# Second-order attention: decayed states read as 32x32 tiles by TensorE instead of as spread 128x128 matrices

## The reference, cut to what matters

```python
def step(carry, qkv):
    S_K, C_QV, G = carry
    C_prev = GAMMA * C_QV
    k_C = jnp.einsum('bhk,bhkv->bhv', k_t, C_prev)
    G = GAMMA * G + k_t[..., :, None] * k_C[..., None, :]
    S_K = GAMMA * S_K + k_t[..., :, None] * k_t[..., None, :]
    C_QV = C_prev + q_t[..., :, None] * v_t[..., None, :]
    S_C = jnp.einsum('bhij,bhjv->bhiv', S_K, C_QV)
    o_t = jnp.einsum('bhk,bhkv->bhv', q_t, S_C - G)
```

## Time and profile before

| | |
|---|---|
| time, median of 3 runs | 3729.63 us |
| span of the profiled execution | 3729.0 us |
| the stage's steady part (1527 to 2762 us) | 1235 us |
| TensorE busy in it | 1226.45 us |
| VectorE, ScalarE, GpSimd busy in it | 599.01, 576.27, 566.54 us |
| TensorE busy over the whole span | 3451.4 us (93%) |

### The profile page before, as it was taken

One profiled execution on the slowest core, in us unless ns is written; L12 is line 12 of the kernel. 1 busy time (PEld: TensorE's weight loads), 2 busy tenths in 40 slices (PEclk: granted clock), 3 DMA queues, 4 the chain that ended last, 5 costly groups with the idle time before them and its releaser, 6 DMA issues. The chain is left out here.

```text
span 3729.0 us, 116380 instructions
## 1 busy us (share of the span) xinstructions
PE 3451.4 (93%) x44854; PEld 3093.9 (83%) x44854; DVE 2374.2 (64%) x6504; ACT 2169.2 (58%) x6623; POOL 1557.1 (42%) x2326
## 2 busy tenths in 40 slices
PE   8939999799839999899999999999988999999998
PEld 8929999677639999798999999999976777777777
DVE  6565555788765554555444444444446899999997
ACT  5546555455346555444444444444444888888896
POOL 5745555200035655344444444444445222222215
PEclk9969999999869999999999999999998999999999
DMA  4153343411153434200000000000000000000002
GB/s 124 47 173 84 86 94 81 121 47 58 52 195 88 94 84 91 77 3 3 3 3 3 3 3 3 3 3 3 3 6 16 2 2 2 2 2 2 2 2 96
DMA packets 137880, 164.78 MB, mean 44 GB/s; under 512 B 11376, under 2 KB 127232, under 8 KB 137344
## 3 DMA queue, kind: packets, MB, share of 16 engines
q1 hardware_dynamic: 112768, 123.79, 10.3%
q0 software_dynamic: 24576, 33.57, 5.3%
HBM read 97.16 MB, written 60.16 MB: 42 GB/s over the span
## 5 line engine op out<-in xcount | busy, mean ns | idle before, releaser
L2374 ACT ACTIVATE wa_S<-wa_S,wa_top 128x256 f32<-128x256 f32 x1024 | 512.2, 507 | 105.9 <-DVE wa_top L2442 104.9
L1956 DVE TENSOR_TENSOR so_raw<-so_rows,so_masks 128x1024 f32<-128x1024 f32 x256 | 313.4, 1224 | 228.0 <-PE so_rows L1655 219.4
L2442 DVE CUSTOM_DVE_ANT_0 wa_S<-wa_bank,wa_band 128x256 f32<-128x256 f32 x1024 | 366.7, 419 | 10.3 <-issue 9.7
L2035 POOL TENSOR_TENSOR so_more<-so_compact,so_head 128x384 f32<-128x384 f32 x224 | 185.2, 827 | 338.6 <-PE so_bankC L1737 308.0
L2291 PE MATMUL wa_bank<-ident,wa_S 128*128 128x128 f32 x2048 | 283.7, 276 | 30.5 <-ACT wa_probT L2381 29.7
L2291 PEld LDWEIGHTS wa_bank<-ident,wa_S 128*128 128x128 f32 x2048 | 229.0, 141 | 73.2 <-ACT wa_S L2374 37.2
L1945 DVE SCALAR_TENSOR_TENSOR so_compact<-so_compact,so_bankX 128x96 f32<-128x96 f32 x192 | 48.8, 254 | 354.9 <-PE so_bankX L1773 354.9
L1870 ACT COPY so_O<-so_bankC 128x128 f32<-128x128 f32 x256 | 68.1, 266 | 308.1 <-PE so_bankC L1737 308.1
L2040 POOL TENSOR_TENSOR so_OT<-so_O,so_OT 128x128 fp32r<-128x128 f32 x256 | 116.9, 457 | 307.7 <-ACT so_OT L1876 307.7
L650 POOL DMA_INDIRECT sum_dram<-y,rows x128 | 223.5, 1746 | 29.5 <-issue 27.2
L728 ACT ACTIVATE m2e_hT<-m_bank,m2e_bias 128x256 fp32r<-128x256 f32 x256 | 127.0, 496 | 152.5 <-PE m_bank L680 147.2
(11 more groups left out here) (449 smaller groups left out, 10114.2 us busy)
## 6 DMA issues: line engine op xcount, KB each, us to landing
m_w_raw<-in_L_ffn_W_dram SPq DMA_DIRECT2D x64, 512.0 KB
sum_dram<-X SPq DMA_DIRECT2D x16, 1024.0 KB, 4.8
X<-sum_dram SPq DMA_DIRECT2D x16, 1024.0 KB, 8.9
X<-in_L_attn_a_x_dram SPq DMA_DIRECT2D x8, 1024.0 KB, 11.4
xn_dram<-m2r_xn SPq DMA_DIRECT2D x16, 512.0 KB, 4.5
sp_gx<-gate_dram SPq DMA_DIRECT2D x64, 128.0 KB, 2.8
xn_dram<-m4r_xn SPq DMA_DIRECT2D x16, 512.0 KB, 4.4
out_dram<-X SPq DMA_DIRECT2D x8, 1024.0 KB, 4.6
```

What stands on the lines that cost most here:

```text
L1956: nc.vector.tensor_tensor(AB[:, t % 2].rearrange("p h m t -> p h (m t)"), rows4[:, :, 0:2 * P], masks[:].rearrange("p m t -> p (m t)")[:, ...
L2035: nc.gpsimd.tensor_tensor(state[:, t % UT], compact[:, t % UT, :, None, :].broadcast_to([P, 3, HG, DK]), head[:, None, :, None].broadcast_ ...
L2374: nc.scalar.activation(S[:, n % 2, z], S[:, n % 2, z], ACT.Exp, bias=top[:, n % 2, z:z + 1], scale=-1.0, accum_out=sums[:, i % 2, SET * c ...
L2442: nc.vector.tensor_tensor_reduce(out=S[:, n % 2, z], in0=bS[g][:, eo * SPAN:(eo + 1) * SPAN], in1=band[:], scale=-(D ** -0.5), scalar=3e38 ...
```

## The change

`spread_state`, the constant `head` and the semaphore `state_ready` go. `state` is now `[P, 2, UT, 3, 32]`: compact, 32 partitions per head, and with two buffers by tile. `update` reads one buffer and writes the other. TensorE takes a 32x32 block of it per head as the stationary operand with `tile_position=(h*32, h*32)` (tile form 32x32).

- `state_to_U` and `state_to_W` become `state_to_UW`: 4 products into `bU` on the diagonal tiles, then 4 into `bC` on the tiles one column group further (`(h*32, (h+1)%4*32)`). To fit this, W is kept with its heads turned by one (`turned_rows`), in `values_to_W`, in `values_to_O` and in `state_products`.
- `state_to_O` becomes 2 x 4 products on the diagonal tiles into `bC`.
- `state_products` splits its 4 products of 64 columns into 8 of 32, since the W part now comes from another head's columns.
- `wo_raw` has a tensor of its own.

```diff
-        more = sb("more", [P, UT * 3 * HG * DK])
-        wo_raw = more[:, 0:UT * HID].rearrange("p (u d) -> p u d", u=UT)
-        state = more[:].rearrange("p (u m h v) -> p u m h v", u=UT, m=3, h=HG)
+        wo_raw = sb("wo_raw", [P, UT, HID])
...
-        compact = sb("compact", [P, UT, 3, DK])
+        state = sb("state", [P, 2, UT, 3, DK])
...
-                def state_of(t, m):
-                    return state[:, t % UT, m].rearrange("p h v -> p (h v)")
-
-                def state_to_U(t):
-                    pe.wait_ge(s_["K_ready"], t + 1)
-                    pe.wait_ge(s_["KQe_ready"], t + 1)
-                    if carries(t):
-                        pe.wait_ge(s_["state_ready"], updates_to(t - UT))
-                        pe.wait_ge(s_["QTg_ready"], carrying_tiles_to(tile(t)))
-                        nc.tensor.matmul(bU[:, 0:P], state_of(t, 0), QTg[:, tile(t) % 2, t % UT], start=True, stop=False)
-
-                def state_to_W(t):
+                def state_of(t, m, h):
+                    return state[head_rows(h), tile(t) % 2, t % UT, m]
+
+                def turned_rows(h):
+                    return head_rows((h + 1) % HG)
+
+                def state_to_UW(t):
+                    pe.wait_ge(s_["S_ready"], updates_to(t - UT))
+                    pe.wait_ge(s_["QTg_ready"], carrying_tiles_to(tile(t)))
                     pe.wait_ge(s_["KTg_ready"], carrying_tiles_to(tile(t)))
-                    nc.tensor.matmul(bC[:, 0:P], state_of(t, 2), KTg[:, tile(t) % 2, t % UT], start=True, stop=False)
+                    for h in range(HG):
+                        nc.tensor.matmul(bU[head_rows(h), 0:P], state_of(t, 0, h), QTg[head_rows(h), tile(t) % 2, t % UT],
+                                         start=True, stop=False, tile_position=(h * DK, h * DK))
+                    for h in range(HG):
+                        nc.tensor.matmul(bC[turned_rows(h), 0:P], state_of(t, 2, h), KTg[head_rows(h), tile(t) % 2, t % UT],
+                                         start=True, stop=False, tile_position=(h * DK, (h + 1) % HG * DK))
 
                 def state_to_O(t):
                     pe.wait_ge(s_["Ug_ready"], carries_to(t))
                     pe.wait_ge(s_["WT_ready"], min(t + 2, NU))
-                    nc.tensor.matmul(bC[:, P:2 * P], state_of(t, 2), Ug[:, t % 2], start=False, stop=False)
-                    nc.tensor.matmul(bC[:, P:2 * P], state_of(t, 1), QTg[:, tile(t) % 2, t % UT], start=False, stop=True
-                                     ).then_inc(s_["O_done"], 1)
+                    for m, of in ((2, Ug[:, t % 2]), (1, QTg[:, tile(t) % 2, t % UT])):
+                        for h in range(HG):
+                            last = nc.tensor.matmul(bC[head_rows(h), P:2 * P], state_of(t, m, h), of[head_rows(h)],
+                                                    start=False, stop=(m == 1), tile_position=(h * DK, h * DK))
+                    last.then_inc(s_["O_done"], 1)
...
-                    for h in range(HG):
-                        nc.tensor.matmul(bX[head_rows(h), HID:HID + 2 * DK], KQe[:, t % 2, 0, head_rows(h)], KW[:, t % 2, :, head_rows(h)],
-                                         start=True, stop=True, tile_position=(0, h * DK))
+                    for m, of in ((0, head_rows), (1, turned_rows)):
+                        for h in range(HG):
+                            nc.tensor.matmul(bX[head_rows(h), HID + m * DK:HID + (m + 1) * DK], KQe[:, t % 2, 0, head_rows(h)],
+                                             KW[:, t % 2, m, of(h)], start=True, stop=True, tile_position=(0, h * DK))
...
-                    old = compact[:, t % UT]
+                    old, to = state[:, tile(t) % 2, t % UT], state[:, (tile(t) + 1) % 2, t % UT]
+                    if t >= UT:
+                        dve.wait_ge(s_["O_done"], carries_to(t - UT))
                     if carries(t):
-                        dve.wait_ge(s_["state_ready"], updates_to(t - UT))
-                        ins = nc.vector.scalar_tensor_tensor(out=old, in0=old, scalar=DECAY, in1=new, op0=ALU.mult, op1=ALU.add)
+                        dve.wait_ge(s_["S_ready"], updates_to(t - UT))
+                        ins = nc.vector.scalar_tensor_tensor(out=to, in0=old, scalar=DECAY, in1=new, op0=ALU.mult, op1=ALU.add)
...
-                def spread_state(t):
-                    pool.wait_ge(s_["S_ready"], updates_to(t))
-                    pool.wait_ge(s_["O_done"], carries_to(t))
-                    nc.gpsimd.tensor_tensor(state[:, t % UT], compact[:, t % UT, :, None, :].broadcast_to([P, 3, HG, DK]),
-                                            head[:, None, :, None].broadcast_to([P, 3, HG, DK]), ALU.mult).then_inc(s_["state_ready"], 1)
```

More of the change, by code:

```diff
@@ L1562, in second_order_attention @@
         masks = sb("masks", [P, 2, P])
-        decay_t, to_end, head = sb("decay_t", [P, P]), sb("to_end", [P, NT]), sb("head", [P, HG])
+        decay_t, to_end = sb("decay_t", [P, P]), sb("to_end", [P, NT])
         xn, xnT = sb("xn", [P, 2, HID]), sb("xnT", [P, 2, HC, 2 * P], F32R)
@@ L1578, in second_order_attention @@
                    QTg_ready KTg_ready row_done AB_ready PT_ready turned K_ready KQe_ready U_done U_ready Ug_ready C_done WT_ready
-                   W_turned W_ready O_done O_ready S_done S_ready state_ready out_done x_ready""".split()
+                   W_turned W_ready O_done O_ready S_done S_ready out_done x_ready""".split()
         s_ = {n: sem(n) for n in names}
@@ L1624, in _ @@
                     sp.dma_start(w_raw[:, n], A[f"L1_attn_a_W{name}"].rearrange("(c p) d -> p c d", p=P)).then_inc(s_[f"{name}_loaded"], 16)
-                sp.dma_start(wo_raw, A["L1_attn_a_Wo"].rearrange("(u p) d -> p u d", p=P)).then_inc(s_["o_loaded"], 16)
-                for to, name in ((masks[:, 0], "upper"), (masks[:, 1], "lower"), (decay_t[:], "decay_t"), (to_end[:], "to_end"), (head[:], "head")):
+                sp.dma_start(wo_raw[:], A["L1_attn_a_Wo"].rearrange("(u p) d -> p u d", p=P)).then_inc(s_["o_loaded"], 16)
+                for to, name in ((masks[:, 0], "upper"), (masks[:, 1], "lower"), (decay_t[:], "decay_t"), (to_end[:], "to_end")):
                     sp.dma_start(to, C[name]).then_inc(s_["loaded"], 16)
@@ L1749, in values_to_W @@
                     for h in range(HG):
-                        last = nc.tensor.matmul(bC[head_rows(h), 0:P], V[:, tile(t) % 2, t % UT, head_rows(h)], AB[:, t % 2, h, 1],
-                                                start=not carries(t), stop=True, tile_position=(0, h * DK))
+                        last = nc.tensor.matmul(bC[turned_rows(h), 0:P], V[:, tile(t) % 2, t % UT, head_rows(h)], AB[:, t % 2, h, 1],
+                                                start=not carries(t), stop=True, tile_position=(0, (h + 1) % HG * DK))
                     return last
@@ L1895, in _ @@
                 act.wait_ge(s_["o_loaded"], 16)
-                nc.scalar.copy(wo[:, 0], wo_raw).then_inc(s_["w_high"], 1)
+                nc.scalar.copy(wo[:, 0], wo_raw[:]).then_inc(s_["w_high"], 1)
                 for n, half, bank in ((0, 0, bJ), (0, 1, bX), (1, 0, bC), (1, 1, bU)):
                     copy_turned(n, half, 0, bank)
-                act.wait_ge(s_["loaded"], 5 * 16)
+                act.wait_ge(s_["loaded"], 4 * 16)
                 for t in range(NU + 2):
@@ L1941, in update @@
                     new = bX[:, HID:HID + 3 * DK].rearrange("p (m v) -> p m v", m=3)
-                    old = compact[:, t % UT]
+                    old, to = state[:, tile(t) % 2, t % UT], state[:, (tile(t) + 1) % 2, t % UT]
+                    if t >= UT:
+                        dve.wait_ge(s_["O_done"], carries_to(t - UT))
                     if carries(t):
-                        dve.wait_ge(s_["state_ready"], updates_to(t - UT))
-                        ins = nc.vector.scalar_tensor_tensor(out=old, in0=old, scalar=DECAY, in1=new, op0=ALU.mult, op1=ALU.add)
-                    else:
-                        if tile(t) >= TB:
-                            dve.wait_ge(s_["state_ready"], updates_to(t - UT))
-                        ins = nc.vector.tensor_copy(old, new)
+                        dve.wait_ge(s_["S_ready"], updates_to(t - UT))
+                        ins = nc.vector.scalar_tensor_tensor(out=to, in0=old, scalar=DECAY, in1=new, op0=ALU.mult, op1=ALU.add)
+                    else:
+                        ins = nc.vector.tensor_copy(to, new)
                     ins.then_inc(s_["S_ready"], 1)
@@ L1975, in _ @@
                 low_xT(0)
-                dve.wait_ge(s_["loaded"], 5 * 16)
+                dve.wait_ge(s_["loaded"], 4 * 16)
                 dve.wait_ge(s_["w_high"], 4)
-                nc.vector.tensor_tensor(wo[:, 1], wo_raw, wo[:, 0].bitcast(F32), ALU.subtract).then_inc(s_["w_ready"], 1)
+                nc.vector.tensor_tensor(wo[:, 1], wo_raw[:], wo[:, 0].bitcast(F32), ALU.subtract).then_inc(s_["w_ready"], 1)
                 for t in range(NU + 4):
@@ L2045, in _ @@
```

(5 more changed lines are left out.)

7 lines of the change are left out of this document (4 added, 3 removed).

## The result

| | before | after |
|---|---|---|
| median of the runs, us | 3730.05 | 3761.15 |
| lowest to highest, us | 3726.96 to 3730.55 | 3760.32 to 3763.87 |
| span of the profiled execution, us | 3729.0 | 3758.5 |
| instructions in TensorE's compiled list, a common carrying step | 198 | 262 |

The ratio is 1.0089 [1.0075, 1.0103]: slower by 31 us, where 7 us faster was forecast. The time lies inside the range that was given, but that is luck: the range reached up to 3770 us for other reasons. It lies on the other side of no change, and the cause is one that had been given a chance of 1 in 20.

The account below looks back on a forecast made before the run. TensorE's own list was taken to bound the kernel. U and W -0.10 and O +0.07 gave -0.03 us a step, times 224 is -6.7 us: forecast 3723 us, range 3690 to 3770.

Parts of the forecast that it names:

- What bounds the kernel: Whole stage: TensorE's own list sets the step; taking 185.2 us of spreads from GpSimd is worth nothing by itself.
- Borders between tile forms: TensorE changing tile form: each border costs 0.10 to 0.12 us, including the two new ones to and from 32x32.
- The rivals with one or both of these free: Borders into and out of 32x32: one free gives 3698 us, both 3674; chance 0.22 (0.12 and 0.10).
- U and W: State reads into two banks: all eight tiles run together, 1.58 + 0.38 = 1.96 us for 2.06, a gain of 0.10.
- the rival of 3766: U and W products run one after the other, 2.15 us instead of 1.96, +43 us; chance 0.20.
- O: State read for O, from leaving 32x128 through the first transpose: 1.06 us for 0.99, a loss of 0.07.
- One bank at a time: Diagonal tiles in U, W and O cannot write one bank together: +441 us, 4164 us; chance 0.04.
- State products: 4 products of 64 columns become 8 of 32: taken as 0, with +0.03 us a step kept for the range.
- Waits: TensorE's KTg wait ahead of U, and VectorE's update waiting for `O_done` of four steps earlier: 0.
- Instructions: TensorE's list, 32 more load-and-multiply pairs on about 86 a step: 0, as long as they are fetched in time.
- The extra instructions come late: Fetching 118 pairs a step for 86 falls behind: 0 to +40 us; chance 0.05.

Follow-up runs that it names:

- same_tiles: The kernel after with W's heads not turned, so head h of U and of W use the same 32x32 tile; 3789.24 us, ratio 1.0168.
- uw_only: Only the compact 32x32 tiles for U and W; O reads a spread copy and state products are four of 64 columns, as before; 3704.87 us, 0.9935.
- border_in: The kernel after with 508 heads' state products split, 3 fillers, chosen to put the block border 20 to 84 instructions in for 203 steps; 3832.2 us, 1.0277.
- phase_28: The kernel after with 28 instructions that do nothing, once, ahead of the first step; 3766.99 us, ratio 1.0104.
- four_wide: The kernel after with state products back at four of 64 columns, 246 instructions a step; 3733.15 us, ratio 1.001.
- border_out: The kernel after with 558 heads' state products split, 4 fillers, chosen to keep the block border out of 20 to 84 in all but 15 steps; 3731.0 us, 1.0013.

## Why the prediction was wrong

- *What bounds the kernel* was right: TensorE's own list, at full clock. GpSimd's 185 us brought nothing.
- *Borders between tile forms.* Right: 0.33 from L1653 to O, 0.33 from O to the first transpose, 0.16 to 0.17 for that one. The rivals with one or both of these free are excluded: 32x128 to 32x32 costs as much as the rest (0.33 from L1653 to O), and so does 32x32 to 128x32 (0.32 from L1730 to L1745 in same_tiles).
- *U and W.* Forecast 1.58 + 0.38; measured 1.61 + 0.38 in the kernel after and 1.58 + 0.37 in uw_only. The eight tiles run side by side in two banks. The Trainium skill (TensorE: Matmul & The Clock Gate, Part 3) would have a weight load overlap running matmuls only where the row group differs, and by it the rival of 3766 would have come true. The trace doesn't agree: tiles of the same rows and other columns start 0.03 us apart.
- *O.* Forecast 1.06; measured 0.33 + 0.57 + 0.17 = 1.07. *One bank at a time* is excluded: four diagonal tiles write one bank side by side. The Trainium skill (TensorEngine Tiling (Array Packing), Gotcha 1) says that different row tiles can't access a bank at the same time; at 0.24 us for eight instructions in one bank the trace doesn't agree, for tiles on partitions of their own.
- *State products.* 0.12 + 0.18 against 0.11 + 0.18, so +0.015 where 0 was taken and +0.03 was the bound. With it the step's sum is about +0.01 instead of -0.03: +2 to +3 us instead of -6.7.
- *Waits* (KTg ahead of U, `O_done` ahead of the update). Right: no new wait for another engine.
- *Instructions.* This step failed: "0, as long as they are fetched in time". The rival "The extra instructions come late" was the true one. It had its price right (0 to +40 us; about 30 measured) and its chance wrong (0.05). The step weighed the mean: 118 pairs take 0.9 of 4.9 us (it also counted too few; a step with twelve projections has 95 pairs before and 127 after, which at its 8 ns are 1.0 us). But the runs show that fetching isn't even. It goes in blocks of 256, and what counts is how many instructions TensorE goes through in the time around a block's arrival. The question to ask was how 262 stands to 256, and it could have been answered: the queue's bytes of the page before, the instructions added by hand, and a count of the rows of a step.

So the stage has 2.8 us for the steps and 30.7 for the stalls and the stretch at half the clock, and the rest of the program 4.0 less, which is the 29.5 between the spans.

## What to carry to other kernels

On an engine that is busy all the time, count its instructions, not only its busy time: per repeat, and against the 256 of a block. A repeat whose count is close to a multiple of 256 keeps the block border in the same place for many repeats, and if that place is a burst of small products, a repeat can lose up to 1.5 us there; another count can end most of it, as 246 for 262 did here. Price a change half by half: here one half (small tiles that use the idle part of the array) is worth 23 us and the other (small tiles where a full product did as well) costs 15, so that the best kernel of this study, 3704.87 us, is half of the change.

## What the runs showed of the hardware

- TensorE's list arrives in transfers of 16,384 bytes, one for each 256 instructions. The one of the stalled step at 2049.1 took 0.92 us, and TensorE resumed 1.46 us after it had landed. In the five runs with such stops (after, border_in, phase_28, same_tiles, four_wide) TensorE goes on 1.2 to 1.6 us after the landing in all 203, and no block is begun sooner than that; what passes in this time isn't shown.
- What keeps a kernel clear of stops is the time between a block's landing and its first instruction. Its least value is 2.6 us in the kernel before, 2.7 in uw_only, 1.5 in border_out and 1.2 in the kernel after.
- In the kernel after, the transfers of blocks at whose border TensorE stops start 88 to 171 instructions ahead of the border, the others mostly 167 to 246 ahead. That fits stalls that keep themselves going, each leaving the next transfer late, but it was read off the positions and not tested by itself. Open are what starts a transfer, and why a run begins with the border at 68 to 84 and not at 43.
- A run of waits that are already met costs TensorE nothing up to 7 in a step, about 0.5 us for ten and 1.0 us for 16, though none of them waits. (Counted in instructions of two waits each.)
- Four 32x32 tiles on the diagonal of one bank (eight instructions in 0.24 us), and eight in two banks (0.38 with the change of form behind them), multiply side by side. Using the same tile twice instead takes 0.19 us more (0.57).
